# A metaformer layer on one Trainium2 core: the last twelve expert groups of the end stage begin two slots later than the first four

## The reference

```python
# attention over channels, then a residual
x = x + conv_ref(ln_c(x), wq, bq, wk, bk, wv, bv, wo, bo, gamma, beta)
# expert part on tokens t = x as (16, 16384, 128); E = 64 experts, K = 8
logits = einsum('bsd,ed->bse', ln_t(t), gate_w) + gate_b
probs = softmax(logits, axis=1)                       # over the tokens
vals, idx = top_k(probs.transpose(0, 2, 1), 8)        # each expert picks 8 tokens
pooled = einsum('bked,bke->bed', gathered, topv)      # weighted sum of its tokens
h = gelu(einsum('ebd,edh->ebh', [pooled, 1], weight1))  # 129 -> 512
out = einsum('ebh,eho->ebo', [h, 1], weight2)           # 513 -> 128
outputs.at[b, idx].add(out * topv)                    # scattered back to the tokens
x = t + outputs
```

## Time and profile before

| | us |
|---|---|
| median of 3 runs | 2166.68 (2166.21 to 2167.01) |
| the profiled execution's own time | 2165.46 |
| its span, first to last instruction | 2163.7 |
| start of the first pooling of the end stage | 1959.1 |
| first scatter of POOL | 2023.1 |
| end of the last scatter instruction | 2157.1 |

### The profile page before, as it was taken

The page is one execution under the profiler, slowest core; times in us unless marked ns, Lnnn a source line. Parts: engine busy times, 40 slices in busy tenths (PEclk is TensorE's granted clock), DMA queues, the critical chain, the costliest instruction groups (busy, mean ns, idle before and its releaser), DMA issues.

```text
span 2163.7 us, 42420 instructions
## 1 busy us (share of the span) xinstructions
PE 1880.8 (87%) x11917; PEld 1289.1 (60%) x11917; DVE 1822.7 (84%) x4612; ACT 1882.8 (87%) x5020; POOL 1941.8 (90%) x2068
## 2 busy tenths in 40 slices
PE   6999999999999999999999999999999986637891
PEld 6866666666666666666666666666666642214561
DVE  4689999999999998989898999999999898623661
ACT  6899999999999999999999999999999977742410
POOL 5799999999999999999999999999999999950377
PEclk9999999999999999999999999999999999755995
DMA  5497888888888888888888888888887676684953
GB/s 194 154 268 212 233 226 213 221 221 227 225 209 227 223 234 221 222 212 225 229 221 215 220 225 234 222 223 218 217 230 218 162 189 161 167 254 121 277 82 31
DMA packets 111068, 447.92 MB, mean 207 GB/s; under 512 B 10575, under 2 KB 52404, under 8 KB 61684
## 3 DMA queue, kind: packets, MB, share of 16 engines
q1 hardware_dynamic: 81140, 302.61, 42.7%
q0 software_dynamic: 29696, 142.61, 34.0%
HBM read 306.78 MB, written 138.41 MB: 206 GB/s over the span
## 4 chain that ended last, share of the span: by engine, by line
ACT 35%; POOL 24%; PE 17%; issue 17%; DVE 4%; ACTq 1%; DMA 1%; POOLq 0%; SPq 0%; DVEq 0%
ACT U L553 14%; POOL U L430 9%; POOL U L435 8%; ACT zT L516 6%; ACT UT L510 5%; PE G L747 4%; ACT LTS L580 3%; PE T L729 3%; ACT LTS L525 3%; POOL zn L451 3%; PE O L680 2%; PE T L736 2%; POOL out_dram L490 2%; POOL U L442 1%; ACT zn L574 1%
## 5 line engine op out<-in xcount | busy, mean ns | idle before, releaser
L553 ACT ACTIVATE U<-xa,nA,rA 128x128 f32<-128x128 f32 x1948 | 803.8, 484 | 2.1 <-issue 1.5
L747 PEld LDWEIGHTS G<-UT 128*128 128x128 f32 x4096 | 536.4, 192 | 226.8 <-issue 225.4
L430 POOL TENSOR_TENSOR U<-U,bet 128x512 f32<-128x512 f32 x512 | 652.2, 1274 | 2.2
L435 POOL TENSOR_TENSOR U<-U,rO 128x512 f32<-128x512 f32 x512 | 533.2, 1041 | 18.9 <-ACT rO L533 18.2
L747 PE MATMUL G<-UT 128*128 128x128 f32 x4096 | 541.4, 275 | 0.0
L680 PE MATMUL O<-U,MT 128*128 128x512 f32 x1024 | 530.5, 600 | 3.5 <-DVE U L933 3.5
L451 POOL TENSOR_TENSOR zn<-U,rZ 128x512 f32<-128x512 f32 x414 | 447.3, 1080 | 10.4 <-ACT rZ L564 10.0
L931 DVE BATCH_NORM_STATS2 stO<-O 128x6 f32<-128x256 f32 x1024 | 386.0, 421 | 52.1 <-PE O L680 51.5
L729 PE MATMUL T<-ident,U 128*128 128x128 f32 x2048 | 323.6, 281 | 118.6 <-ACT UT L510 108.1
L729 PEld LDWEIGHTS T<-ident,U 128*128 128x128 f32 x2048 | 224.1, 142 | 317.7 <-issue 312.8
L949 DVE BATCH_NORM_STATS2 stA<-xa 128x6 f32<-128x256 f32 x1024 | 385.7, 424 | 31.2 <-DMA xa<-in_x 27.7
(11 more groups left out here) (151 smaller groups left out, 1667.2 us busy)
## 6 DMA issues: line engine op xcount, KB each, us to landing
xa<-in_x SPq DMA_DIRECT2D x128, 1024.0 KB, 6.3
U<-in_x POOLq DMA_DIRECT2D x128, 1024.0 KB, 10.7
out_dram<-U SPq DMA_DIRECT2D x128, 1024.0 KB, 8.5
U<-in_L_ffn_weight SPq DMA_DIRECT2D x112, 256.0 KB
LTS<-in_L_ffn_weight SPq DMA_DIRECT2D x16, 256.0 KB
xa<-out_dram,UT POOLq DMA_INDIRECT x64
out_dram<-U,UT POOLq DMA_INDIRECT x64
zT<-in_L_ffn_weight SPq DMA_DIRECT2D x1, 128.0 KB
```

The lines of the kernel that those rows point to most:

```text
L430: gp.tensor_tensor(rows(a, i), rows(a, i), bet_b, ALU.add).then_inc(S["gb"], 1)
L435: gp.tensor_tensor(rows(a, i), rows(a, i), rO[:, i // 2 % 2, i % 2 * TI:(i % 2 + 1) * TI].unsqueeze(2).to_broadcast([P, TI, W]), ALU.mult) ...
L553: last = sc.activation(utile(a, i, j), xa[:, k % XR, h * W:(h + 1) * W], ACT.Identity, scale=rA[:, k % 2, h:h + 1], bias=nA[:, k % 2, h:h ...
L747: last = te.matmul(G[:, 0:P], v, v, start=(i == 0 and j == 0), stop=(i == NI - 1 and j == TI - 1))
```

## The change

The slot loop gets two more slots. A helper `group(t)` says which group a lag refers to: groups 0 to 3 as before, none for 4 and 5, and `t - 2` from slot 6 on. So layer1 has no group in slots 4 and 5, turn1 none in 5 and 6, layer2 none in 6 and 7, turn2 none in 7 and 8, codes none in 10 and 11, outputs and combine none in 11 and 12. Groups 4 to 15 keep their lags among each other and lie two slots later than before. No instruction is added or removed, apart from three activation table loads that the order of ACT no longer needs.

```diff
-SLOTS = NG + 7
+
+PAUSE = 2
+SLOTS = NG + 7 + PAUSE
...
+        def group(t):
+
+            g = t if t < 4 else t - PAUSE
+            return g if 0 <= g < NG and (t < 4 or g >= 4) else None
...
             for t in range(SLOTS):
-                if t < NG and t % 4 == 0:
-                    pooled(t // 4)
-                if t < NG:
-                    act.wait_ge(R_["h"], t + 1)
-                    wait(act, R_["trh"], t - 1)
-                    sc.activation(Hs[:, t % 2, :], O[t % 2][:, :], ACT.Gelu).then_inc(R_["ge"], 1)
-                if 0 <= t - 2 < NG:
-                    g = t - 2
+                if (g := group(t)) is not None:
+                    if g % 4 == 0:
+                        pooled(g // 4)
+                    act.wait_ge(R_["h"], g + 1)
+                    wait(act, R_["trh"], g - 1)
+                    sc.activation(Hs[:, g % 2, :], O[g % 2][:, :], ACT.Gelu).then_inc(R_["ge"], 1)
+                if (g := group(t - 2)) is not None:
...
             for t in range(SLOTS):
-                if t < NG and t % 4 == 0:
-                    pooling(t // 4)
-                if t < NG:
-                    layer1(t)
-                if 0 <= t - 3 < NG:
-                    turn2(t - 3)
...
+                if (g := group(t)) is not None:
+                    if g % 4 == 0:
+                        pooling(g // 4)
+                    layer1(g)
+                if (g := group(t - 3)) is not None:
+                    turn2(g)
...
```

More of the change, by code:

```diff
@@ L637, in _ @@
                     sc.activation(OUTs[:, g % 2, :], O[2][:, 0:W], ACT.Copy).then_inc(R_["ou"], 1)
[L638 to L641, removed]
+                if (g := group(t)) is not None and g % 4 in (1, 2) and g // 4 + 1 < Q:
+                    scales(g // 4 + 1, g % 4 - 1)
+                if (u := group(t - 7)) is not None:
                     act.wait_ge(R_["cmm"], u + 1)
@@ L840, in _ @@
             for t in range(SLOTS):
-                if t < NG and t % 4 == 0:
-                    pooling(t // 4)
-                if t < NG:
-                    layer1(t)
-                if 0 <= t - 3 < NG:
-                    turn2(t - 3)
[L847 to L856, removed]
+                if (g := group(t)) is not None:
[4 more added lines that the diff above has]
+                    turn2(g)
+                if (g := group(t - 7)) is not None:
+                    outputs(g)
+                if (g := group(t - 1)) is not None:
+                    turn1(g)
+                if (g := group(t - 6)) is not None:
+                    codes(g)
+                if (g := group(t - 2)) is not None:
+                    layer2(g)
+                if (g := group(t - 7)) is not None:
+                    combine(g)
         @block.vector
@@ L1114, in _ @@
             for t in range(SLOTS):
-                if 0 <= t - 3 < NG:
-                    g = t - 3
+                if (g := group(t - 3)) is not None:
                     q = g // 4
@@ L1124, in _ @@
                                    .to_broadcast([P, NB, K, 4])).then_inc(R_["ott"], 1)
-                if 0 <= t - 7 < NG:
-                    u = t - 7
+                if (u := group(t - 7)) is not None:
                     q, g = divmod(u, 4)
@@ L1131, in _ @@
                                      TQ[:, q, 4 * g:4 * g + 4, 0].unsqueeze(2).to_broadcast([P, 4, W]), ALU.mult).then_inc(R_["v"], 1)
-                if 0 <= t - 1 < NG:
-                    g = t - 1
+                if (g := group(t - 1)) is not None:
                     dve.wait_ge(R_["trh"], g + 1)
@@ L1136, in _ @@
                     ve.tensor_copy(HTs[:, g % 2, :], T1[:, :]).then_inc(R_["ht"], 1)
[L1137 to L1140, removed]
+                if (u := group(t - 6)) is not None:
+                    equal(u)
+                if (g := group(t)) is not None and g % 4 in (1, 2) and g // 4 + 1 < Q:
+                    prepare(g // 4 + 1, g % 4 - 1)
 _INS = ["x", "L0_conv_wq", "L0_conv_bq", "L0_conv_wk", "L0_conv_bk", "L0_conv_wv", "L0_conv_wo", "L0_conv_gamma",
```

## The result

The changed kernel takes 2180.99 us in the median of four runs (2179.67 to 2183.20), against 2166.85 for the kernel before (2166.21 to 2171.32). The ratio is 1.0058 with a 95% interval of 1.0042 to 1.0073: slower by 0.6%. Two later series gave 1.0041 (1.0027 to 1.0056) and 1.0055 (1.0039 to 1.0070). The forecast of 2170.2 had the sign but not the size, and the range of 2165.2 to 2174.2 doesn't hold the result.

What follows compares the result with a forecast made beforehand. PE's arrival at combine(5) was taken to bound the kernel, through the C copy of group 5 and POOL's fixed tail. Stalls +0.4, clock +2.1 and +1.0 gave +3.5 us: median 2166.68 to 2170.2, range 2165.2 to 2174.2.

Steps and rivals of the forecast that it cites:

- The reading of the end: End of kernel: PE reaching combine(5) sets the C copy of group 5, then a fixed POOL tail of 83.0 us.
- the PE work in the sum: PE ahead of combine(5): the same work stands before it in both orders, so the change is zero.
- The clock, second quarter: PE around the second quarter's pooling: moved work falls into the half-clock stretch, +2.1 us, bounds 0 and 5.5.
- The clock, third and fourth quarter: PE around the later two poolings: third unchanged, last pooling partly slower, +1.0 us, bounds -1.6 and +3.3.
- the first rival: Fourth quarter's pooling: the clock stays low through it, over 6 us; +7.3 in all, 2174.0 us, chance 0.24.
- Stalls: PE's waits in the emptied slots and by prepare, less the 5.4 us of before: +0.4 us together.
- The emptied slots: Slots 4 and 5 on PE: layer2 and turn2 wait on copy and spread without cover, +1.6 us, bounds 0.7 and 2.6.
- the fourth quarter's prepare: Slots 11 and 12: prepare on DVE delays what PE needs, stalls of 3.0 us, bounds 2.1 and 5.
- The third quarter's: Prepare in slots 7 and 8 delays V of group 1 and the spread of group 4: 1.2 us, bounds 0 and 3.3.
- Table loads of ACT: ACT loses three table loads, in slots that stall anyway: 0, down to -1.3 us each if one were bare.
- The third rival: Second quarter's pooling runs at full clock, under 4 us: -4.0 in all, 2162.7 us, chance 0.05.
- The fourth: Rival: POOL's scatter is the bound throughout, so starting 5 us earlier ends 5 us earlier, 2161.7 us, chance 0.03.

Runs made afterwards that it cites:

- e1: The changed source with the pause of empty slots set to 0, giving every engine the order of the kernel before: 2170.75 us, 1.0002 to before.
- e4: The kernel before with unread transposes of the identity on PE, in stalls and in each pooling but the first: 2163.30 us, 0.9970 to before.
- e8: The changed kernel with prepare and scales of the third quarter in slots 5 and 6 instead of 7 and 8: 2156.96 us, 1.0025 to before.
- e7: The changed kernel with a pause of one empty slot in place of two: 2156.71 us, 1.0025 to before.
- e5: The changed kernel with unread transposes in stalls, and four after every fourth product of each pooling but the first: 2146.00 us, 0.9975 to before.
- e10: As e6, with six transposes after every pooling in place of five, and six more in slots 4, 8 and 12: 2143.50 us, 0.9964 to before.
- e6: As e4, but four transposes after every fourth product of each pooling but the first and five at its end: 2144.43 us, 0.9966 to before.

## Why the prediction was wrong

The reading of the end was right: the C copy of group 5 sets the end, the tail behind it is 83.0 us, the earlier first quarter gains nothing, the PE work in the sum is unchanged (966 instructions), and POOL's idle time grows to 23.3 us, counted as in the prediction, within its 20 to 25. The terms of the sum:

- *The clock, second quarter*, forecast +2.1 with an upper bound of 5.5. This step failed. I took the work of slots 4 and 5 at half clock, with some of it spared, and assumed that the clock would be back after layer1 of group 4 as before. It came back a whole layer1 later, at 2018.4: the low stretch grew by 13.8 us, with 12.2 us more of PE's work in it, which is worth 6.1. Not only the moved work was slow, but `codes(0)` (2.07 us, not 1.08) and layer1 of group 5 too. The repeats bear this out: 17.1 us without the pause, 37.5 and 27.3 with it.
- *The clock, third and fourth quarter*, forecast +1.0, bounds to 3.3. Measured 6.9 us more at half clock, worth 3.4. Of this 3.4 us (worth 1.7) were in the third quarter, which is within what e1 shows without any pause. The rest is the last pooling, 6.85 us in all three profiles with the pause: what the first rival named, and I gave it 0.24. Its price of +7.3 was still too small, by 2.5 us for the clock of the second quarter and by 2.0 for the stalls.
- *Stalls*, forecast +0.4, measured +2.4. The emptied slots were right (1.6 forecast, 1.66 measured), the fourth quarter's prepare nearly (3.0, 3.42). The third quarter's was taken at 1.2 and cost 2.78: of its two parts, 0.6 each, the wait for V of group 1 came to 0.56, but the one for the spread of group 4, in slot 9, to 2.22.
- *What lies ahead of the end stage*, forecast at nothing: 3.7 us in the compared profiles, by chance as far as e1 to e4 show.
- *Table loads of ACT*, forecast at 0 on the ground that three fall away, as the section on the change has it too: none does. Both traces hold 42420 instructions, with 7, 6 and 6 table loads in the end stage. The term of 0 was right all the same.

The stretch grew by 11.35 us, against 3.5: 2.4 by stalls and 8.9 by PE's busy time, which is the clock. With the 3.7 us this makes the 15.0. Over all profiles it grew by 10.7, so the step was wrong beyond the luck of one run; the 3.7 us are what chance added.

I had bounded the clock by the work that moves and one layer1 more. The bound should have been the time until the clock is back, and with the pause that came later; which piece of work brings it back the runs leave open. The third rival, a fast pooling of the second quarter, is out: it took 7.01 us again. The fourth is out too: in e8 POOL began 6 us before e7 (2005.12, 2011.11), and the two take the same time.

What POOL's start shows I also had wrong: 2027.46, not 2016 to 2020. `combine(0)` was done at 2021.1, but on ACT its copy stands behind `scales` of the third quarter, which wait for prepare on DVE; it began at 2025.84. It cost nothing here.

## What to carry to other kernels

Before emptying slots of a pipeline on PE, look at the granted clock around them and ask what will bring it back; here 3.6 us of other work put into a stretch at half clock came with a stretch twice as long. A kernel whose end hangs on one engine's arrival gains nothing by giving its last queue an earlier start: here 44 scatters behind the C copy of group 5 take 83.0 us in either order. Where the clock falls over necessary but light PE work, unread full transposes in its stalls and gaps can pay for themselves, and can narrow the spread of the times; try amounts, since too few leave the clock to fall and those ahead of a stage delay it.

## What was not expected of the hardware

- The same order of instructions took 113.6 or 118.5 us in the end stage (kernel before, e1), with mean clocks of 0.77 and 0.75. The steps of the clock don't fall at the same instruction in each run. A single profile's low stretches are one draw; I had read them as fixed.
- A 128x8 cast on DVE took 0.17 us in the median and 2.31 us at most before, 2.76 after. The long ones are not random in place: at 288 us it was 0.5 or 2.8 us in six profiles, at 1861 to 1864 always 2.2 to 2.3. Each of the six that took over 0.5 us in these two traces ended 0.03 or 0.04 us behind an instruction of POOL: at 289.00 (POOL at 288.97) before, at 291.17 (291.14, two POOL instructions later) in the changed kernel. That such a cast waits for POOL is a guess from this; no run tests it.
- What makes a pooling bring the clock down is left open. PE was busy without a gap in it (7.01 us at 0.50), and transposes between its products kept the clock up in e5 and e10, but not in each run of e6.
